# Attention block: q·k products halved by adding DMAs, x's rows added by DMA, six product buffers, and eight pipeline stages

## The reference

```python
# block 1: group norm and 1x1 convolution, then attention ACROSS THE 8 IMAGES at each of 4096 pixels
t = conv1x1(groupnorm(x)) + pe[image]
q2, k2, v2 = three projections of layernorm(t)            # 8 heads of 8 channels
attn = softmax(q2 . k2 / sqrt(8))                         # per pixel and head: 8 x 8
t = attn @ v2 @ wout.T + bout + t
m = (layernorm(t) @ w1.T + b1) * gelu(t @ w2.T + b2) @ w3.T + b3
x = conv1x1(m + t) + cob + x
# block 2: three steps
for _ in range(3):
    x = x + conv3x3(relu(conv3x3(x, w1) + b1), w2) / 3 + b2 / 3
out = relu(x)
```

## Time and profile before

| | |
|---|---|
| median of 3 runs | 1139.01 us (1138.61 to 1140.38) |
| profiled execution, span from first to last instruction | 1136.3 us |
| busy over the span | PE 1071.2 (94%), DVE 1039.7 (92%), ACT 652.5 (57%), POOL 510.7 (45%) |
| attention block | 44.65 to 604.73 us |
| three conv steps | 604.73 to 1136.3 us |

### The profile page before, as it was taken

The page is one execution under the profiler, slowest core; times in us unless marked ns, Lnnn a source line. Parts: engine busy times, 40 slices in busy tenths (PEclk is TensorE's granted clock), DMA queues, the critical chain, the costliest instruction groups (busy, mean ns, idle before and its releaser), DMA issues. The chain is left out here.

```text
span 1136.3 us, 21019 instructions
## 1 busy us (share of the span) xinstructions
PE 1071.2 (94%) x7238; PEld 601.7 (53%) x7238; DVE 1039.7 (92%) x1475; ACT 652.5 (57%) x1525; POOL 510.7 (45%) x422
## 2 busy tenths in 40 slices
PE   4269999999999999999999999999999999999996
PEld 3156787778777777777653333333333333333331
DVE  5459999999999999999988999999999999999996
ACT  4568889888888888888743233253244242342333
POOL 5134564456445544554452424435345344444440
PEclk9999999999999999999999999999999999999998
DMA  8110111111111111110000000030001100030003
GB/s 303 54 37 21 39 29 35 32 39 29 33 35 38 29 31 38 38 29 20 20 20 1 1 1 1 1 75 1 1 1 34 41 1 1 1 74 1 1 1 74
DMA packets 87545, 35.83 MB, mean 32 GB/s; under 512 B 70210, under 2 KB 86851, under 8 KB 86931
## 3 DMA queue, kind: packets, MB, share of 16 engines
q1 hardware_dynamic: 85634, 33.81, 11.1%
q0 software_dynamic: 768, 0.33, 0.2%
q10 hardware_dynamic: 1040, 0.35, 0.1%
HBM read 26.09 MB, written 8.39 MB: 30 GB/s over the span
## 5 line engine op out<-in xcount | busy, mean ns | idle before, releaser
L1173 ACT ACTIVATE y<-banks,cols 128x1024 f32<-128x1024 f32 x96 | 110.3, 1208 | 259.8 <-PE banks L1165 259.8
L900 POOL TENSOR_TENSOR rstd<-var,half 128x8 f32<-128x8 f32 x32 | 80.8, 2526 | 216.5 <-DVE var L755 216.5
L1155 PE MATMUL banks<-mixed_h,cwp 128*128 128x512 f32 x384 | 177.6, 605 | 0.0
L1155 PE MATMUL banks<-early,cwp 128*128 128x512 f32 x372 | 169.2, 602 | 0.5 <-PEq L420 0.5
L1456 POOL TENSOR_TENSOR early<-xs 128x256 f32<-128x256 f32 x95 | 77.1, 811 | 160.1 <-DVE xs L1204 160.1
L1181 DVE TENSOR_TENSOR y<-y,banks 128x512 f32<-128x512 f32 x192 | 119.9, 682 | 15.2 <-ACT y L1173 15.0
L558 PE MATMUL banks<-consts,early 128*128 128x128 f32 x1024 | 133.2, 279 | 0.0
L1189 DVE TENSOR_TENSOR y<-y,banks 128x512 f32<-128x512 f32 x192 | 124.4, 685 | 8.7 <-PE banks L1165 6.5
L577 PE MATMUL banks<-consts,prod 128*128 128x128 f32 x1024 | 128.2, 273 | 2.8 <-DVE prod L526 2.1
L1155 PEld LDWEIGHTS banks<-mixed_h,cwp 128*128 128x128 f32 x384 | 69.0, 189 | 107.9 <-issue 107.9
L558 PEld LDWEIGHTS banks<-consts,early 128*128 128x128 f32 x1024 | 114.3, 144 | 18.8 <-issue 18.1
(11 more groups left out here) (184 smaller groups left out, 1868.8 us busy)
## 6 DMA issues: line engine op xcount, KB each, us to landing
xs<-in_x SPq DMA_DIRECT2D x4, 2048.0 KB, 16.5
xa<-in_x SPq DMA_DIRECT2D x32, 256.0 KB, 2.8
xr<-in_x SPq DMA_DIRECT2D x64, 128.0 KB, 2.8
out_y<-xs SPq DMA_DIRECT2D x32, 256.0 KB, 4.5
cw<-in_L_conv_w POOLq DMA_DIRECT2D x2, 144.0 KB, 3.9
consts<-in_consts ACTq DMA_DIRECT2D x1, 192.0 KB
group<-in_consts SPq DMA_DIRECT2D x1, 64.0 KB
w1n<-in_L_conv_w ACTq DMA_DIRECT2D x1, 64.0 KB
```

The costliest lines, as they stand in the source:

```text
L900: pool.tensor_tensor(rstd1[:, :], var1[:, :], top["half"][:, :], ALU.pow).then_inc(rstd1_done, 1)
L1155: pe.matmul(psum[PSUM_PAIR[v, q, j]][i][:, :, :], weights(v, i, j).rearrange("p n o -> p (n o)"), mixed[v][i][:, s0:s0 + WIDE, j, :], star ...
L1173: act.activation(pairs(y[i][q][:, :, :]), m1, ACT.Identity, bias=cols[:, (6, 8)[v]:(7, 9)[v]]).then_inc(m1_out[i][q], 1)
```

## The change

1. `dve_p1` is as before, but block b of tile t goes to one of six buffers, slot (4t + b) mod 6. `pool_e_add`, new, is a DMA issued by GpSimd that adds channels 4 to 7 of a block to channels 0 to 3 (128 partitions of 2 KB, SBUF to SBUF, `accum_op=add`): four per tile, 128 in all. `pe_scores_t` then transposes four products per block and no longer eight.
2. `dve_x` and `sp_xr` with its buffers are gone. `act_x`, new, is two ScalarE activations per tile (PSUM to `xs`, with the bias column). `pool_residual`, new, is two DMAs issued by GpSimd per tile that add x's rows from memory to `xs` (64 partitions, 8 pieces of 256 bytes on each), 64 in all.
3. `prod2` has five slots for two-image blocks; `qkv` and `tt` have five buffers, `z1` three.
4. Each engine's order is new, with 39 iterations (`STAGES = 8`). TensorE does `scores_t` of tile t - 3, `av` of t - 5 (block 0 of t - 4), the last projections of t - 6; ScalarE does `act_t`, squares and raw of tile t in iteration t; DVE does p1 of t - 1, p2 of t - 3, z1 and tn2 of t - 4, gated of t - 5. GpSimd's in-order list is bias, e_add, residual, rstd1, e_add, rstd2, e_add, e_add.
5. Semaphores are per block, and at the end of the attention block GpSimd waits for the last residual DMAs.

```diff
-        RING = 4
+        STAGES = 8
+        T_RING, QKV_RING, Z1_RING = 5, 5, 3
+        P1_SLOTS, P2_SLOTS = 6, 5
+        OWN_QKV = QKV_RING - 3
...
+        prod1 = [top["early"][0][:, HD * P * k:HD * P * (k + 1)].rearrange("p (e s) -> p e s", e=HD) for k in range(4)]
+        prod1 += [sb(f"prod1_{k}", [P, HD, P])[:, :, :] for k in range(4, P1_SLOTS)]
+        prod2 = [sb(f"prod2_{k}", [P, 2, B * C]) for k in range(P2_SLOTS)]
...
+        def p1_slot(t, b):
+            return prod1[(DUOS * t + b) % P1_SLOTS]
+
+        def p2_slot(t, b):
+            return prod2[(DUOS * t + b) % P2_SLOTS]
+
+        def user(t, b, slots):
+
+            return divmod(DUOS * t + b - slots, DUOS)
...
+            wait(pe, e_added[b][t % 2], 16 * (t // 2 + 1))
+            for e in range(HD // 2):
+                m = pe.matmul(b2[:, P * b:P * (b + 1)], p1_slot(t, b)[:, e, :], ident,
+                              start=(e == 0), stop=(e == HD // 2 - 1), is_transpose=True)
+            m.then_inc(scoresT_mm[b], 1)
...
+        def pool_e_add(pool, t, b):
+
+            wait(pool, p1_dve[b], t + 1)
+            v = p1_slot(t, b)
+            pool.dma_start(v[:, 0:HD // 2, :], v[:, HD // 2:HD, :], accum_op=ALU.add).then_inc(e_added[b][t % 2], 16)
+
+        def act_x(act, t, d):
+
+            wait(act, cow_mm, t + 1)
+            act.activation(x_view(t, d), x_psum(d), ACT.Identity, bias=cols[:, 4:5]).then_inc(x_done[d], 1)
+
+        def pool_residual(pool, t):
+
+            for d in range(2):
+                wait(pool, x_done[d], t + 1)
+            for r in range(2):
+                wait(pool, residual[r], 16 * t)
+                pool.dma_start(xs[half(r), :, t, 1:1 + HW], x_rows[:, :, 2 * t + r, :], accum_op=ALU.add)\
+                    .then_inc(residual[r], 16)
+
+        def dve_p1(dve, t, b):
             wait(dve, biased, t + 1)
-            wait(dve, scoresT_mm, DUOS * (t - 1) + b + 1)
-            p1_product(dve, k, b).then_inc(p1_dve, 1)
+            last, old = user(t, b, P1_SLOTS)
+            wait(dve, scoresT_mm[old], last + 1)
+            p1_product(dve, t, b).then_inc(p1_dve[b], 1)
...
-        def dve_x(dve, t, k, d):
-
-            if isinstance(t, int):
-                dve.wait_ge(xr_in[k % 2], 32 * (t // 2 + 1))
-            else:
-                dve.wait_ge(xr_in[k % 2], (t - k % 2) * 16 + 32)
-            wait(dve, cow_mm, t + 1)
-            dve.scalar_tensor_tensor(x_view(t, d), x_psum(d), cols[:, 4:5], xr_view(k, d), ALU.add, ALU.add).then_inc(x_done[d], 1)
...
+        def pe_iteration(pe, t, tiles):
+            if tiles[5]:
+                pe_av(pe, t - 5, 3)
+            if tiles[6]:
+                pe_rstd2(pe, t - 6)
+            if tiles[5]:
+                pe_av(pe, t - 5, 1)
+                pe_av(pe, t - 5, 2)
+            if tiles[6]:
+                pe_a(pe, t - 6)
+            if tiles[5]:
+                pe_z1(pe, t - 5)
+            if tiles[0]:
+                pe_t(pe, t)
+            if tiles[5]:
+                pe_center(pe, t - 5)
+                pe_g(pe, t - 5)
+            if tiles[0]:
+                pe_qkv(pe, t, 0)
+            if tiles[5]:
+                pe_var2(pe, t - 5)
+            if tiles[3]:
+                pe_scores_t(pe, t - 3, 0)
+                pe_scores_t(pe, t - 3, 1)
+                pe_scores_t(pe, t - 3, 3)
+                pe_scores_t(pe, t - 3, 2)
+            if tiles[6]:
+                pe_out(pe, t - 6)
+            if tiles[0]:
+                pe_qkv(pe, t, 1)
+            if tiles[6]:
+                pe_cow(pe, t - 6)
+            if tiles[3]:
+                pe_scores(pe, t - 3)
+            if tiles[4]:
+                pe_av(pe, t - 4, 0)
+        def act_iteration(act, t, tiles):
+            if tiles[0]:
+                act_t(act, t)
+            if tiles[5]:
+                act_square2(act, t - 5)
+                act_centered(act, t - 5)
+                act_gelu(act, t - 5, 1)
+            if tiles[0]:
+                act_squares(act, t, 0)
+                act_raw(act, t, 0)
+            if tiles[3]:
+                act_scores_t(act, t - 3)
+            if tiles[1]:
+                act_scale(act, t - 1)
+            if tiles[5]:
+                act_rrep(act, t - 5)
+            if tiles[6]:
+                act_x(act, t - 6, 1)
+            if tiles[0]:
+                act_squares(act, t, 1)
+            if tiles[6]:
+                act_x(act, t - 6, 0)
+            if tiles[5]:
+                act_gelu(act, t - 5, 0)
+            if tiles[0]:
+                act_raw(act, t, 1)
+            if tiles[4]:
+                act_z(act, t - 4)
+            if tiles[3]:
+                act_exp(act, t - 3)
+        def dve_iteration(dve, t, tiles):
+            if tiles[0]:
+                dve_var1(dve, t)
+            if tiles[4]:
+                dve_z1(dve, t - 4)
+                if t - 4 == TILES - 1:
+                    outer_ahead(dve, ((1, 0), (1, 1)))
+            if tiles[5]:
+                dve_gated(dve, t - 5, 0)
+                if t - 5 == TILES - 2:
+                    outer_ahead(dve, ((0, 0), (0, 1)))
+            if tiles[3]:
+                dve_sum(dve, t - 3)
+            if tiles[5]:
+                dve_gated(dve, t - 5, 1)
+            if tiles[3]:
+                dve_reciprocal(dve, t - 3)
+            if tiles[1]:
+                dve_p1(dve, t - 1, 1)
+            if tiles[3]:
+                dve_attn(dve, t - 3)
+            if tiles[1]:
+                dve_p1(dve, t - 1, 0)
+            if tiles[4]:
+                dve_var2(dve, t - 4)
+            if tiles[3]:
+                dve_p2(dve, t - 3, 0)
+                dve_p2(dve, t - 3, 3)
+                dve_p2(dve, t - 3, 1)
+            if tiles[2]:
+                dve_max(dve, t - 2)
+            if tiles[3]:
+                dve_p2(dve, t - 3, 2)
+            if tiles[2]:
+                dve_shift(dve, t - 2)
+            if tiles[4]:
+                dve_tn2(dve, t - 4)
+                if t - 4 == TILES - 1:
+                    outer_ahead(dve, ((0, 2), (1, 2)))
+            if tiles[1]:
+                dve_p1(dve, t - 1, 3)
+                dve_p1(dve, t - 1, 2)
+        def pool_iteration(pool, t, tiles):
+            if tiles[1]:
+                pool_bias(pool, t - 1)
+            if tiles[2]:
+                pool_e_add(pool, t - 2, 2)
+                if t - 2 == TILES - 1:
+                    inner_ahead(pool, ((1, 0), (1, 1)))
+            if tiles[7]:
+                pool_residual(pool, t - 7)
+            if tiles[0]:
+                pool_rstd1(pool, t)
+            if tiles[1]:
+                pool_e_add(pool, t - 1, 1)
+            if tiles[4]:
+                pool_rstd2(pool, t - 4)
+                if t - 4 == TILES - 2:
+                    inner_ahead(pool, ((0, 0), (0, 1)))
+                if t - 4 == TILES - 1:
+                    inner_ahead(pool, ((0, 2), (1, 2)))
+            if tiles[1]:
+                pool_e_add(pool, t - 1, 0)
+                pool_e_add(pool, t - 1, 3)
+        def sp_iteration(sp, t, tiles):
+            if 2 <= t + 1 < TILES:
+                sp_xa(sp, t + 1)
...
+            for r in range(2):
+                pool.wait_ge(residual[r], 16 * TILES)
```

More of the change, by code:

```diff
@@ L452, in attention_block @@
         z = sb("z", [P, N])
-        z1 = [sb(f"z1_{k}", [P, N]) for k in range(2)]
+        z1 = [sb(f"z1_{k}", [P, N]) for k in range(Z1_RING)]
         cen2 = sb("cen2", [P, N])
@@ L711, in act_scale @@
                 wait(act, raw_out[g], t + 1)
+            v = qkv[t % QKV_RING]
             for i in range(B):
-                act.activation(qkv[k][:, i, :], qkv[k][:, i, :], ACT.Identity, scale=rstd1[:, i:i + 1]).then_inc(scaled_out, 1)
+                act.activation(v[:, i, :], v[:, i, :], ACT.Identity, scale=rstd1[:, i:i + 1]).then_inc(scaled_out, 1)
         def act_scores_t(act, t):
-            wait(act, scoresT_mm, DUOS * (t + 1))
+            for b in range(DUOS):
+                wait(act, scoresT_mm[b], t + 1)
             wait(act, scores_mm, t)
@@ L724, in act_z @@
         def act_z(act, t):
-            wait(act, av_mm, DUOS * (t + 1))
+            for b in range(DUOS):
+                wait(act, av_mm[b], t + 1)
             wait(act, z1_mm, t)
@@ L796, in dve_attn @@
             wait(dve, rden_done, t + 1)
-            wait(dve, p2_dve, DUOS * t)
+            for b in range(DUOS):
+                wait(dve, p2_dve[b], t)
             r = rden[:, :].unsqueeze(2).broadcast_to([P, C, B])
@@ L872, in free_for @@
             if i == 0:
-                wait(eng, scoresT_mm, DUOS * TILES)
-            else:
-                wait(eng, p2_dve, DUOS * (TILES - 1))
+                for b in range(DUOS):
+                    wait(eng, scoresT_mm[b], TILES)
+            else:
+                for b in range(DUOS):
+                    wait(eng, p2_dve[b], max(t + 1 for t in range(TILES) if t % QKV_RING >= OWN_QKV))
             wait(eng, edges_zeroed, 1)
         def written(eng, c):
```

(13 more changed lines are left out.)

259 lines of the change are left out of this document (71 added, 188 removed).

## The result

The changed kernel takes **1207.37 us** (median of 4 runs), the kernel before 1139.6. I had forecast 1113. The span of the profiled execution went from 1136.3 to 1205.2 us, 68.9 more where I had 26 less.

The account below looks back on a forecast made before the run. A ring of waits through GpSimd's adding DMAs was to set iterations at 15.3 us, just above ACT and DVE. Filling 65 + 27 iterations 413 + draining 56 = 534 against 560; 1139 - 26 = 1113 us, range 1098 to 1150.

Parts of the forecast that it names:

- the part on the bias: GpSimd's bias, started while DVE's p1 of block 2 runs, takes 2.85 us, with 3.44 as upper end.
- DVE's work, 14.8: DVE's steady iteration falls from 16.27 us by 0.78 (x), 0.4 (gaps) and up to 0.3 (z1) to 14.8.
- ACT 14.85 and PE 14.5: Work per iteration: ScalarE 14.19 plus 0.66 for two x activations; TensorE at most 14.5 us after losing 16 transposes.
- The ring: Once-per-iteration wait loop: p1 of block 3, e_add, bias, e_add of block 2, PE, DVE, p1 again; 15.3 us, sets the time.
- L: Time from issue to landing of the e_add of block 2, taken as 3.9 us.
- The DMAs' issue: GpSimd's six issues per iteration cost 0.6 us per e_add and 0.8 per residual; 12.5 of 15 us, engine not full.
- my third rival: Dear residual issue: late from 1.45 us each; at 2.7 each, iterations of 16.25 and 1138 us; chance 0.11.
- GpSimd's rows exceed 1.5 us: Sign in GpSimd's DMA rows, expected at 0.6 and 0.8 us, that the forecast is wrong.
- Filling, 65: Start of the attention block: first p1 at 66 us instead of 61.07, five iterations in 65 us.
- Draining, 56: From iteration 32 to the conv steps: 33.7 to the last p2, 17.0, 4.2 for the last residuals, 1.15; together 56 us.
- late landing: Rival: e_add lands later than a plain copy; gain gone at 4.75 us, 1179 us at 6; chance 0.20.
- if the bias or rstd stretch under the products: Sign that the forecast is wrong: GpSimd's bias or rstd lengthened by more than one of DVE's products.

Follow-up runs that it names:

- e2: Changed kernel with var1 still DVE's first step, but written as tensor_reduce instead of tensor_scalar, without the 1e-5; 1144.96 us, 1.0049 of the kernel before.
- e4: e1 without pool_e_add: PE transposes all eight products of a block and waits for p1 itself; 1218.64 us, 1.0697 of the kernel before.
- e6: e1 with pool_residual moved behind rstd2 in GpSimd's list; 1134.68 us, 0.996 of the kernel before.
- e1: Changed kernel with DVE's var1 moved from first in its iteration to behind reciprocal; 1144.57 us, 1.0051 of the kernel before.
- e3: Changed kernel with z1 moved ahead of var1 in DVE's iteration; 1162.56 us, 1.0203 of the kernel before.
- e8: Changed kernel with PE repeating pe_center's four matmuls three times while it waits for z1; 1185.47 us, 1.0403 of the kernel before.
- e9: e7 with separate semaphores for residual DMAs of odd and even tiles; 1125.25 us, 0.9884 of the kernel before.
- e7: e6 with residual DMAs one iteration sooner and the last tile's x made by DVE from rows SP loaded; 1127.27 us, 0.9894 of the kernel before.
- the repeated e7: e7 unchanged, measured again beside e9 on the same chip in the same rounds; 1128.9 us, 0.9914 of the kernel before.
- e5: e1 with only the DMA in pool_e_add removed: GpSimd still waits for each p1, PE transposes all eight products; 1176.97 us, 1.033 of the kernel before.

## Why the prediction was wrong

**The step that failed** is in the part on the bias: "behind it come var1, z1, gated and sum, of which none has two SBUF inputs (...). So I take 2.35 + 0.5 = 2.85 us". I asked what DVE would do to the bias, and only by one of the ways in which the two engines exclude each other. I didn't ask what the bias would do to DVE, and so put var1's wait at nothing in "14.8 us of DVE work per iteration". The bias took 2.68 us, less than I took, and var1 paid 2.36 us instead (2.53 for 0.17), in each iteration. The Trainium skill, page "SBUF — State Buffer", section "Who interferes with whom", says in the same list from which I took the rule on two inputs that `tensor_scalar` can run in a mode that takes both of VectorE's ports, that the one of the two engines which is issued first then keeps the shared ports and the other blocks wholly, and that `tensor_reduce` on this chip never contends. By that rule, the traces agree: var1 takes 2.53 us in the changed kernel, the reduction in e2 0.15, and a product with two SBUF inputs issued just behind the bias in e4 3.16.

What follows from it, term by term:
- *DVE's work, 14.8.* Right but for this: 14.76 in e6. With 2.36 more it is 17.1, the iteration of the changed kernel. DVE is in order, so z1 and PE wait too; I had even counted on up to 0.3 us of gain because z1 stands behind var1. e1, e2 and e3 each take away all or part of the wait by another edit, and the time follows.
- *ACT 14.85 and PE 14.5.* 14.67 and 14.64.
- *The clock.* Not in my sum at all. Seven iterations went to 20.38 us by TensorE's low clock, behind a pause of 2.46 to 2.74 us; e8 prices it at 22 us. Of the 72.5 us by which the 27 iterations exceed 413, 22.6 are this, and 49.9 are 1.85 per iteration, 17.1 against 15.3.
- *The ring, 11.4 + L, and L.* L is 3.7, and the ring doesn't set the time: DVE's max doesn't wait in a steady iteration of the changed kernel. It shows in longer iterations of e6. Its true length stays open, between nothing that is seen at 15.09 and a late e_add at 15.83. That e6's mean iteration, 15.26, is close to my 15.3 is luck: the 15.3 was the ring's length, and e6's regular iteration is DVE's 14.76 and its wait for PE.
- *The DMAs' issue.* By the ends of the records an e_add takes 0.83 to 0.91 us against 0.6, and a residual about 1.2 against 0.8 (2.39 for two in e1, 2.37 in the changed kernel; 1.17 where four stand alone in e9). That is above my figures and below the 1.45 from which my third rival said that it's late. The records themselves are longer (median 1.74 us for a residual), so my sign "GpSimd's rows exceed 1.5 us" was one that a row can show without the cost being there. It was late, in e1: ScalarE's scale waited 0.46 us for rstd1, and what held DVE was rstd2 and tn2, further down the same list. From e1 to e6 it is 0.73 us per regular iteration and 14.6 in all. The changed kernel hides it: GpSimd idles 4.42 us per iteration there.
- *Filling, 65.* First p1 at 66.5 against 66. Of the 11.6 us missed, some 5 are the lock (e1's second z1 comes 4.9 us sooner than the changed kernel's); DVE also idles 4.4 us before the third var1, and the granted clock is 0.93 on the mean here, in e1 0.95, before the change 1.00. The rest wasn't taken apart.
- *Draining, 56.* Of the 7.9 us missed, 3.2 lie ahead of the last p2 (36.9 us from iteration 32 on, where I had 33.7; 2.6 of them a wait of z1 for PE) and 0.9 between it and the last x. The last x is ready at 661.5, and the conv steps start 9.2 us later, where I had 5.35. I took 4.2 us for the last residual. Its two issues are 2.30, another 5.0 pass until it has landed, and they stand behind another pair that waits for a landing as they do. Counted from the 29th z1 on, e7 got 8.3 us back at this place (60.1 us against e6's 68.4) and e9 1.6 more (against the repeated e7). The conv steps are 3.0 us longer since their start is at the low clock: in their first 10 us the mean granted clock is 0.71, behind PE's 8.3 us of idling, and their first four matmuls take 3.75 us; in e9, after 1.22 us of idling, 1.96.

The slower rival that I priced, late landing, came nearest to the measured time (1179) for a cause that wasn't there: the e_adds landed as I had taken it. Of the signs that I named, "if the bias or rstd stretch under the products" pointed at the right pair of engines and at the wrong one of the two: the bias took 2.68 us and rstd1 2.43 by the ends of the records.

With var1 elsewhere, the residuals out of the ring and the tail mended, the same adding DMAs give 1125 us. What each of the change's two ideas gives there isn't shown: the adding DMAs were priced in e1's order alone (1.0 us per iteration, e5), no run loads x's rows by SP for all tiles in the new order, and for the last tile e7 and e9 went back to loaded rows.

## What to carry to other kernels

When a step is moved on VectorE, look at what GpSimd runs at that moment, and look at it from both sides: a `tensor_scalar` of 8 numbers from SBUF to SBUF cost nearly as much here as the GpSimd instruction that it fell under (2.53 us under 2.68), and the profile shows it as busy time, so compare an instruction's minimum with its median. A wait that seems useless may be what keeps two such instructions apart (e4 and e5). A pause of TensorE in each iteration is to be priced with the clock, and a DMA issued by GpSimd with the place it takes in GpSimd's list, above all ahead of a result for which others wait. GpSimd's records overlap, so what an issue costs is read from the ends of consecutive records.

## What the runs showed of the hardware

- A DVE `tensor_scalar` of 128x8 from SBUF to SBUF that is issued while GpSimd runs a `tensor_tensor`: 2.53 us instead of 0.17. `tensor_reduce` of the same elements: 0.15. A DVE product with two SBUF inputs issued 0.29 us behind the bias: 3.16 instead of 1.22. A `scalar_tensor_tensor` that reads PSUM and one SBUF tile, issued 0.19 us behind the bias (e3): 0.74, as elsewhere.
- GpSimd is taken up for 0.83 to 0.91 us by the issue of an adding DMA of 256 KB in 2 KB pieces, and for about 1.2 by one of 128 KB in 512 pieces of 256 bytes, by the ends of the records. From SBUF to SBUF the first lands in 3.4 to 4.2 us by the median of the run, the second, from memory, in 3.7 to 4.8, while SP's plain load of 256 KB takes 2.7 to 3.5.
- Pauses of 2.3 to 2.9 us of PE in each iteration of 17.1 us let the clock fall in seven iterations and not in the others, and pauses of 2.46 stand before iterations of both kinds; with pauses of 1.0 to 1.6 us (e8) and 0.58 (e3) it didn't fall. What decides in which iterations it falls, the runs don't show.
